# x1 of the second layer multiplied out transposed, 512 tokens at a time, in place of token tiles that are transposed afterwards

## What is computed

```python
q = _lin_lora(x, W[0], A[0], B[0]); k = ...; v = ...      # 4-bit codes looked up and scaled, plus rank 16
attn = (q + k + v) / 3.0
x1 = x + _lin_lora(attn, W[3], A[3], B[3])
g = _lin_lora(x1, Wg, Ag, Bg)
u = _lin_lora(x1, Wu, Au, Bu)
h = jax.nn.silu(g) * u                                     # 1024 x 1792
x = x + attn_block(x)                                      # attn_block returns x1 + d, d = _lin_lora(h, Wd, Ad, Bd)
x = _layernorm(x)
```

## Time and profile before

| | us |
|---|---|
| median of 3 runs | 661.75 (661.51 to 661.8) |
| the profiled execution's own time | 661.55 |
| span of that execution | 659.7 |
| PE busy | 642.2 (97%) |
| DVE busy | 394.1 (60%) |
| ACT busy | 384.2 (58%) |
| POOL busy | 67.5 (10%) |
| mean granted clock of TensorE | 0.996 |

### The profile page before, as it was taken

One profiled execution on the slowest core, in us unless ns is written; L12 is line 12 of the kernel. 1 busy time (PEld: TensorE's weight loads), 2 busy tenths in 40 slices (PEclk: granted clock), 3 DMA queues, 4 the chain that ended last, 5 costly groups with the idle time before them and its releaser, 6 DMA issues.

```text
span 659.7 us, 8518 instructions
## 1 busy us (share of the span) xinstructions
PE 642.2 (97%) x3232; PEld 473.7 (72%) x3232; DVE 394.1 (60%) x622; ACT 384.2 (58%) x528; POOL 67.5 (10%) x117
## 2 busy tenths in 40 slices
PE   9999999999999999999999999999999999999995
PEld 6655455554547778888888888886777888888874
DVE  2778867749688859676766527324675221215566
ACT  3877778866787777766767236213456333226532
POOL 1122213302231000000000000001111000000012
PEclk9999989999999999999999999999999999999999
DMA  6870287522323324332421003038000222100002
GB/s 226 294 269 33 85 267 192 160 80 64 100 99 108 103 70 141 102 108 77 126 79 31 1 0 129 1 113 365 0 5 29 80 97 67 61 1 0 1 32 97
DMA packets 25015, 64.19 MB, mean 97 GB/s; under 512 B 5478, under 2 KB 10022, under 8 KB 24079
## 3 DMA queue, kind: packets, MB, share of 16 engines
q1 hardware_dynamic: 23486, 61.50, 28.9%
q10 hardware_dynamic: 1488, 2.15, 1.0%
HBM read 58.90 MB, written 4.73 MB: 96 GB/s over the span
## 4 chain that ended last, share of the span: by engine, by line
PE 88%; DVE 4%; ACT 4%; issue 2%; POOL 1%; POOLq 0%; ACTq 0%; DVEq 0%
PE bank L1004 19%; PE bank L1083 8%; PE bank L1082 8%; PE bank L991 7%; PE bank L992 7%; PE bank L993 7%; PE bank L766 4%; PE bank L843 4%; PE bank L597 3%; PE bank L716 2%; PE bank L679 1%; PE bank L690 1%; PE bank L631 1%; PE bank L622 1%; PE bank L751 1%
## 5 line engine op out<-in xcount | busy, mean ns | idle before, releaser
L1191 ACT ACTIVATE line<-line 128x1024 f32<-128x1024 f32 x87 | 91.2, 1049 | 0.1
L991 PE MATMUL bank<-xh,wh 128*128 128x512 f32 x224 | 87.5, 391 | 0.0
L992 PE MATMUL bank<-xl,wh 128*128 128x512 f32 x224 | 87.4, 390 | 0.0
L993 PE MATMUL bank<-xh,wl 128*128 128x512 f32 x224 | 87.3, 390 | 0.0
L1004 PE MATMUL bank<-wh,xh 128*128 128x512 f32 x192 | 76.0, 396 | 0.2 <-DVE xl L2082 0.2
L1004 PE MATMUL bank<-wh,xl 128*128 128x512 f32 x192 | 74.9, 390 | 0.0
L2165 DVE SCALAR_TENSOR_TENSOR arena<-bank,ff_s,arena 128x512 f32<-128x512 f32 x28 | 21.0, 751 | 72.9 <-PE bank L1083 63.7
L2082 DVE TENSOR_TENSOR xl<-arena,xh 128x1024 fp32r<-128x1024 f32 (+1 forms) x26 | 29.6, 1141 | 35.2 <-ACT xh L1508 35.0
L1082 PE MATMUL bank<-xh,wh 128*128 128x512 f32 x128 | 50.2, 392 | 0.0
L1083 PE MATMUL bank<-xl,wh 128*128 128x512 f32 x128 | 49.9, 390 | 0.0
L1508 ACT ACTIVATE xh<-arena 128x1024 fp32r<-128x1024 f32 (+1 forms) x26 | 25.6, 991 | 41.3 <-PE bank L1004 34.8
(11 more groups left out here) (211 smaller groups left out, 1276.2 us busy)
## 6 DMA issues: line engine op xcount, KB each, us to landing
codes<-in_c_gu SPq DMA_DIRECT2D x14, 512.0 KB, 3.6
scales<-in_s_gu SPq DMA_DIRECT2D x28, 256.0 KB, 3.8
codes<-in_t_gu SPq DMA_DIRECT2D x8, 512.0 KB, 4.2
codes<-in_c_dn SPq DMA_DIRECT2D x7, 512.0 KB, 5.1
scales<-in_s_dn SPq DMA_DIRECT2D x14, 256.0 KB, 4.0
fold<-in_t_dn SPq DMA_DIRECT2D x1, 3584.0 KB, 16.6
scales<-in_t_gu SPq DMA_DIRECT2D x6, 512.0 KB, 3.7
x<-in_x SPq DMA_DIRECT2D x2, 1024.0 KB, 6.0
```

Source lines behind the costliest of these rows:

```text
L991: pe.matmul(dst, wh[:, s, c:c + P], xh[:, k, cols], start=(k == 0), stop=False)
L992: pe.matmul(dst, wh[:, s, c:c + P], xl[:, k, cols], start=False, stop=False)
L993: last = pe.matmul(dst, wl[:, s, c:c + P], xh[:, k, cols], start=False, stop=(k == KD - 1))
L1191: nc.scalar.activation(below(slot), below(slot), ACT.Prelu, bias=bias, scale=scale, alpha=alpha).then_inc(bent, 1)
```

## The change

x1 is made transposed. The weight is the stationary operand and 512 tokens are the moving one: `x1_T(tg, c)` gives part c of the width for half tg of the tokens, 12 matmuls, into one bank that ACT and DVE read straight into `xh` and `xl`. The copy, the addition and the transposes of x1 go. The rows of x1 are brought back later: `x1_rows_of(b)` multiplies `xh` and `xl` of x1, as stationary operands, with the 128x128 identity in float32r (`unit_r`), into the bank where the down products of tile b are then added: 8 matmuls of 128 columns for each of 8 tiles. `ffn_W(7)` moves to step t = 5. The first two hidden parts of the down stage are worked in halves of the tokens.

```diff
+X1_BANK = ((4, 5, 0, 1), (7, 6, 4, 5))
+FIRST_DN = 2
...
+        unit_r = sb("unit_r", [P, P], F32R)
-        ones = sb("ones", [KD, P])
+        ones = folded_m[0:KD, 0:P]
...
-            def attention_out(t):
...
+            def x1_T(tg, c):
+
+                if tg == 0 and c == 0:
                     pe.wait_ge(m_low, KD)
+                    pe.wait_ge(xl_ready, NT // 2)
+                elif tg == 0 and c == 2:
+                    pe.wait_ge(lmT_ready, NT)
+                elif c == 0:
+                    pe.wait_ge(xl_ready, NT)
+                elif tg and c >= 2:
+                    pe.wait_ge(xl_ready, NT + c - 1)
+                cols, dst = slice(tg * 512, (tg + 1) * 512), bank[X1_BANK[tg][c]][:, :]
                 for k in range(KD):
+                    high, low = m_hi[:, k, c * P:(c + 1) * P], m_lo[k][:, c * P:(c + 1) * P]
+                    pe.matmul(dst, high, xh[:, k, cols], start=(k == 0), stop=False)
+                    pe.matmul(dst, high, xl[:, k, cols], start=False, stop=False)
+                    last = pe.matmul(dst, low, xh[:, k, cols], start=False, stop=(k == KD - 1))
                 last.then_inc(x1_ps, 1)
...
-                if t + 2 < NT - 1:
+                if t + 2 < NT:
                     ffn_W(t + 2)
-                elif t == NT - 1:
-                    ffn_W(t)
...
+                if t == NT - 1:
+                    x1_T(0, 0)
                 lora_out(t)
                 if t >= 2:
                     x_T(2, t - 2)
-            for t in range(2):
-                attention_out(t)
-                x_T(2, NT - 2 + t)
...
+            x1_T(0, 1)
+            x_T(2, NT - 2)
+            x1_T(0, 2)
+            x_T(2, NT - 1)
+            x1_T(0, 3)
+            x1_T(1, 0)
+            gu_lora(0)
+            x1_T(1, 1)
+            x1_T(1, 2)
+            gu_lora(1)
+            x1_T(1, 3)
+
+            def x1_rows_of(b):
+
                 if b == 0:
+                    pe.wait_ge(lora_added, NF)
+                    pe.wait_ge(fold_kept, NF)
+                elif b >= 2 and b % 2 == 0:
+                    pe.wait_ge(h_ready, TG * NF + 1 + b // 2)
+                for k in range(KD):
+                    for m in (xh, xl):
+                        last = pe.matmul(late_bank(b)[:, k * P:(k + 1) * P], m[:, k, b * P:(b + 1) * P], unit_r[:, :], start=(k == 0 and m is xh), stop=False)
+                last.then_inc(x1_rows, 1)
...
+                    if j == NF - 1:
+                        for b in range(NT // 2) if tg == 0 else range(NT // 2, NT - 2):
+                            x1_rows_of(b)
...
-            for j in range(DN_LAST):
+            dn_half(0, 0)
+            for b in range(NT - 2, NT):
+                x1_rows_of(b)
+            dn_half(1, 0)
+            for j in range(FIRST_DN):
+                dn_half(j, 1)
+            for j in range(FIRST_DN, DN_LAST):
                 dn_group(j)
...
+            def x1_T_out(tg, c):
+
+                if c == 0:
+                    act.wait_ge(x1_ps, KD * (tg + 1))
+                nc.scalar.activation(xh[:, c, tg * 512:(tg + 1) * 512], bank[X1_BANK[tg][c]][:, :], ACT.Copy).then_inc(xt_ready, 1)
...
             b_high(0)
             b_high(1)
-            x1_copy(3)
-            x1_T_out(1)
+            for c in range(KD):
+                x1_T_out(0, c)
+            gu_hi(0, 0)
             act.wait_ge(in_gu[1], 16)
             bend_first(C_GU + 1, gu_slot(1))
...
             bend_second(C_GU + 1, gu_slot(1), (scaled, C_GU))
...
+            for n in range(2, LEAD):
+                bend_below(C_GU + 1, gu_slot(1), n)
+            for c in range(KD):
+                x1_T_out(1, c)
             gu_hi(1, 1)
             gu_first_bends(0, 2, 1, (w_ready, 1))
             b_high(2)
...
+            def x1_T_low(tg, c):
...
+                nc.vector.tensor_tensor(xl[:, c, cols], bank[X1_BANK[tg][c]][:, :], f32(xh[:, c, cols]), ALU.subtract).then_inc(xl_ready, 1)
...
             gu_join_above(0, 0)
             b_lower(0)
             b_lower(1)
-            x1_add(2)
-            x1_low(1)
+            nc.vector.tensor_copy(unit_r[:, :], ident[:, :])
+            dve.wait_ge(kb_out, 16 * KD)
+            nc.vector.memset(ones, 1.0)
             gu_to_scale(0, 0, 0)
...
+            for c in range(KD):
+                x1_T_low(0, c)
             gu_lora_add(0, 0)
...
             gu_low(0, 0)
...
             gu_join_above(1, 1)
...
+            for c in range(KD):
+                x1_T_low(1, c)
             gu_to_scale(1, 1, 0)
...
             gu_lora_add(1, 1)
             gu_low(1, 1)
```

More of the change, by code:

```diff
@@ L335, in t_code, with dn_ready @@
             return codes[:, j % SLOTS, :] if j % SLOTS < RING else scales[:, j % SLOTS - RING, :].bitcast(I32)
+        def dn_ready(j):
+            return place(j) + 1 + FIRST_DN
         def place(j):
@@ L396, in decoder_kernel @@
         ag_ps, lm_ready, lm_ps, lmT_ready, f0_ps = (sem(n) for n in ("ag_ps", "lm_ready", "lm_ps", "lmT_ready", "f0_ps"))
-        af_ps, af_added, m_ps, m_high, m_low, x1_ps, x1_ready, x1_sum = (sem(n) for n in ("af_ps", "af_added", "m_ps", "m_high", "m_low", "x1_ps", "x1_ready", "x1_sum"))
+        af_ps, af_added, m_ps, m_high, m_low, x1_ps, x1_rows = (sem(n) for n in ("af_ps", "af_added", "m_ps", "m_high", "m_low", "x1_ps", "x1_rows"))
         gate_ps, up_ps, sil_ready, h_ready = (sem(n) for n in ("gate_ps", "up_ps", "sil_ready", "h_ready"))
@@ L567, in _ @@
             for used, dst, src, done in ((KQ_F, kqT, kq_dram, in_kq), (BETA_F, beta[0:KD, :], beta_dram, in_kq), (CTX_F, ctx1, i["ctx"], in_ctx1)):
-                sp.wait_ge(dn_low, down_ready(used - 1) if used < NF else NF + 1)
+                sp.wait_ge(dn_low, dn_ready(used - 1) if used < NF else NF + FIRST_DN)
                 sp.dma_start(dst, src).then_inc(done, 16)
@@ L943, in gu_lora @@
                 last.then_inc(lora_made, 1)
-            def x1_T(b):
-                pe.wait_ge(x1_ready, b + 1)
-                if b == 0:
[L949 to L967, removed]
+            x1_T(0, 1)
[10 more added lines that the diff above has]
+            def x1_rows_of(b):
+                if b == 0:
+                    pe.wait_ge(lora_added, NF)
[6 more added lines that the diff above has]
+                last.then_inc(x1_rows, 1)
             def gu_tile(s, j):
@@ L1009, in dn_products, with dn_half @@
                 h, l, wh_j, wl_j = hidden_part(xh, j), hidden_part(xl, j), dn_part(wh, j), dn_part(wl, j)
-                return down_products(late_bank(b)[:, :], b, (h, h, l), (wh_j, wl_j, wh_j), j == 0, j == NF - 1)
+                return down_products(late_bank(b)[:, :], b, (h, h, l), (wh_j, wl_j, wh_j), False, j == NF - 1)
             def dn_landed(j):
-                pe.wait_ge(dn_low, down_ready(j))
+                pe.wait_ge(dn_low, dn_ready(j))
                 pe.wait_ge(dn_wlow, place(j) + 1)
+            def dn_half(j, half):
+                pe.wait_ge(dn_low, FIRST_DN * half + j + 1)
+                if not half:
+                    pe.wait_ge(dn_wlow, j + 1)
+                for b in range(half * NT // 2, (half + 1) * NT // 2):
+                    last = dn_products(j, b)
+                if half:
+                    last.then_inc(hu_used, 1)
             def dn_group(j):
-                if j:
-                    dn_landed(j)
+                dn_landed(j)
                 for b in range(NT):
[L1022 to L1030, removed]
                     last = dn_products(j, b)
@@ L1058, in x_scores @@
                     pe.matmul(late_bank(b)[:, 0:P], xT[:, k, t], kqT[:, k, t], start=(k == 0), stop=False)
-                pe.matmul(late_bank(b)[:, 0:P], ones[:, :], beta[0:KD, t], start=False, stop=True).then_inc(x_ps, 1)
+                pe.matmul(late_bank(b)[:, 0:P], ones, beta[0:KD, t], start=False, stop=True).then_inc(x_ps, 1)
             def x_probT(b):
@@ L1437, in _ @@
                 unit_bends(u, h)
-            x1_copy(1)
             x_T_out(3 * NT - 1, dst=xh)
[L1440 to L1444, removed]
+            for u, h in half_plan(3, NT, 1) + half_plan(3, NT + 1, 0) + half_plan(3, NT + 1, 1):
                 unit_bends(u, h)
@@ L1518, in _ @@
             silu(1, NF - 1, 0)
-            act.wait_ge(up_ps, 2 * NF + 1)
-            hidden_hi(hidden_part(xh, 0), 0, HALVES[0], dn_hi)
+            act.wait_ge(x1_rows, NT // 2)
             act.wait_ge(fold_kept, NF)
-            dn_weight_hi(0)
+            for j in range(FIRST_DN):
+                hidden_hi(hidden_part(xh, j), j, HALVES[0], dn_hi)
+                dn_weight_hi(j)
             silu(1, NF - 1, 1)
-            act.wait_ge(up_ps, 2 * NF + 2)
-            hidden_hi(hidden_part(xh, 0), 0, HALVES[1], dn_hi)
-            for j in IN_ORDER[1:]:
+            act.wait_ge(x1_rows, NT)
+            for j in range(FIRST_DN):
+                hidden_hi(hidden_part(xh, j), j, HALVES[1], dn_hi)
+            for j in IN_ORDER[FIRST_DN:]:
                 act.wait_ge(h_ready, TG * (j + 1) + 4)
```

(22 more changed lines are left out.)

48 lines of the change are left out of this document (1 added, 47 removed).

## The result

| | before | after |
|---|---|---|
| median, us | 661.77 | 670.92 (670.03 to 671.56, 4 runs) |
| ratio, 95% interval | | 1.0139 (1.0119 to 1.0159) |
| the profiled execution's own time | 661.55 | 670.03 |
| its span | 659.7 | 668.2 |
| PE busy | 642.2 | 646.6 |

The median is 0.7 us from the forecast of 671.6 and inside the stated range. Of before's four times one, 1660.4 us, is far off the rest; it moves the median by 0.02 us.

The account below looks back on a forecast made before the run. The prediction took PE, working 97% of the span, as the bound, to be checked against the supply of weights. It summed 661.55 + 2.4 (supply and clock) + 7.6 (identity products) = 671.6 us, range 665 to 678.5.

Parts of the forecast that it names:

- Before x1: From lora_T(5) to x_T(2, 7): new waits sum to 2.1 us, like those removed; x_T(2, 7) starts at 209.6 us.
- The x1 stage on PE: 32 transposes go, 3.5 us in all; gate/up starts at 225.4 instead of 229.57, 4.2 us earlier.
- The supply: ACT's and DVE's weight chain into gate/up comes 1.2 us later; PE waits 1.1 us in tile 0, stands 4.8 after it.
- The clock: At gate/up tile 1 PE's stand makes TensorE's clock fall once, 1.8 us lost; net 2.4 us with the supply's shift.
- The row at 85 us: Ground for the fall: clock 0.50 in 85 to 86 us, eight matmuls taking 5.40 us against 3.60.
- Identity products: 64 F32R matmuls of 128 columns added to PE for x1's rows, without cover: 0.118 us each, 7.6 us.
- Gate/up and down: Later gate/up is PE's, so the shift is carried, not made up; the down stage adds nothing.
- The clock stays up: Rival at gate/up tile 1: no clock fall, the shift is 1.2 us, total 670.4 us; chance 0.28.
- PE's saving is kept: Rival for the x1 stage: supply comes before PE, -4.9 us, total 664.3 us; chance 0.10.
- Slow narrow F32R: Rival for the identity products: they cost 14.9 us instead of 7.6, total 678.9 us; chance 0.12.
- products at the price of their columns: Rival: identity products cost only their columns, 3.7 us; chance 0.05 with PE's saving kept, 0.07 with the forecast supply.
- Not slower: Rival: identity products cost 3.7 us; 660.4 us with PE's saving kept (chance 0.05), 666.4 with the forecast supply (0.07).

Follow-up runs that it names:

- e9: e5 with attention_product before ffn_W from step t = 4 on, not step 3, and m_high_of(3) before norm_tail; 660.31 us, ratio 0.9979.
- e3: Changed kernel with b_high(2) ahead of tile 2's bends on ACT and b_lower(2) ahead of join_above on DVE; 671.56 us, ratio 1.0151.
- e4: Changed kernel with the six bends of weight tile 1 ahead of gu_hi(0, 0) on ACT; 666.99 us, ratio 1.0096.
- e5: e4 plus tile 2's bends started before x1's second-half copies, b_high(2) before gu_hi(1, 1), b_lower(2) before gu_join_above(0, 2); 663.14 us, ratio 1.0024.
- e2: Changed kernel with 19 unread 512-column matmuls on PE in the stand at the end of gate/up tile 0; 669.98 us, ratio 1.0130.
- e0: Changed kernel run again unaltered, on the same chip as e5, e7 and e8; 671.29 us, ratio 1.0142.
- e1: Changed kernel with 32 of the 64 identity products, those of x1's low parts left out; 667.14 us, ratio 1.0089.
- e7: e5 with attention_product before ffn_W in all steps and m_high_of(3) before norm_tail; 664.14 us, ratio 1.0041.
- e8: Kernel before the change with attention_product before ffn_W in steps 3 and 4; 664.59 us, ratio 1.0052.

## Why the prediction was right, step by step

**Before x1.** Forecast: waits of 0.8, 0.9 and 0.4 us, `x_T(2, 7)` 2.9 us later. Measured 0.77, 0.54 and 0.48, and 2.5 us. In e9 the first two are gone and nothing takes their place, so they were PE's own; the third is still there in e9 and was not tried.

**The x1 stage on PE.** Forecast 15.8 us from `x_T(2, 7)` to gate/up; measured 16.00. One transpose at 0.108 and a block of 12 at 2.8 us were right.

**The supply.** Forecast: 26.0 us from `x_T(2, 7)` to `gu_hi(1, 1)`. Measured 233.70 - 207.51 = 26.19. The copy to `unit_r` and the memset, which had no row, took 0.23 and 0.17, taken as 0.3. Forecast waits 1.1 and 4.8, measured 0.89 and 4.59. Counted from `lora_T(5)`, the last event that both kernels share, `gu_hi(1, 1)` comes 1.1 us later than before (53.4 us against 52.3), forecast 1.2. This has two parts that the prediction runs together: `x_T(2, 7)` is 2.5 us later, and from there the chain is 1.5 us shorter than before's 27.7 us. The blocks of x1 work on ACT and DVE therefore did not lengthen this chain; they kept it from coming forward with PE, which reaches gate/up 4.3 us earlier. e3 (the stand moves), e4 (it shrinks when ACT's list changes) and e5 (it goes) show that the order of the lists is what holds the supply back.

**The clock.** Right that it falls, and e2 shows that the stand is what makes it fall. The size was a guess from one row (1.8 us of slow matmuls, 1.2 net): `gu_lora(2)` to `down_lora` grew by 2.2 us in one execution and 0.9 in e0. The term was 1.0 us too small for the one and 0.3 too large for the other; how long the clock stays down once PE works again differs between executions. The row at 85 us was a weak ground for the fall itself: PE is busy through 82 to 84 us there, so no stand comes just before it, and in the changed kernel's first execution the same matmuls ran without a fall (1.00 in 84 to 88 us). e2 ties the fall to the stand, that row does not.

**Identity products.** Forecast 0.118 each, 7.6 us; measured 0.112 and, over the rest of the program, 7.0 us (e1: 0.11 each). The transposes (0.108) were the nearer row. What the prediction only argued, that the load of the stationary tile sets this price, a row of its own supports: the 16 one-column matmuls of the earlier trace rows each have a load of their own (least, median and longest ns of one, then the first and the last start):

```profile
L729 PEld LDWEIGHTS bank<-picked,folded x16: 190/192/192, 81.5 to 83.2; 128*128 128x128 f32 x16
L729 PE MATMUL bank<-picked,folded x16: 169/250/250, 81.6 to 83.2; 128*128 128x1 f32 x16
```

With 0.25 us for one they start (1.84 - 0.25)/15 = 0.106 us apart: one column costs as much as 128. These are float32; no run changes the columns of an F32R product alone. The figure of the Trainium skill ("TensorE: Matmul & The Clock Gate", "Back-to-back issue gap"), about 81 ns for load and 128-column matmul, does not hold for the float32 and F32R operands here, with their 0.106 to 0.112 us.

**Gate/up and down.** Nothing is made up or lost there, as forecast: `down_lora` to the end differs by 7.0 us, which the products alone (7.2 by their distance) account for.

**The rivals.** "The clock stays up", 670.4 us, is nearer to the median of 670.92 (0.5 us) than the forecast (0.7); the time could not have told them apart, the trace does. "PE's saving is kept" forecast 664.3; e5, which lets it through, gives 663.14. Slow narrow F32R and products at the price of their columns both fall to e1. The sum of 666.4 under "Not slower" leaves out the forecast's own clock term; with the supply as forecast it would be 661.55 + 2.4 + 3.7 = 667.7.

**The sum.** From `lora_T(5)` to `down_lora` of tile 1 the forecast adds 2.4 us; the first execution added 3.3, e0 2.0. The products were forecast 0.6 too dear. So the mechanism is right, and that the total is right to 0.7 us is in part luck: errors of up to 1 us lie on both sides. The comparison has a flaw as well: the sum was made against an execution that had the early clock fall. Without it the first execution of the changed kernel costs 8.5 + 1.8 = 10.3 us more; e0, which has the fall like before, costs 9.4 more (669.1 against 659.7); the forecast was 10.0 and the medians differ by 9.2.

## What to carry to other kernels

When PE is nearly always busy, look at how much slack its suppliers have before counting a saving on PE: follow their lists from the last common event and compare the two arrival times. An instruction that waits, on an engine that works through its list in order, holds everything behind it, even where the engine's total work falls; here ACT idled 4.8 us with ready work behind (moving six bends into that time returned 3.9 us), and the order of both lists put right returned 8. When each small matmul brings a stationary tile of its own, don't price it by its columns: here 128 columns cost half of 512, and one column as much as 128, so summing by identity products is dear.

## What was not expected of the hardware

A stand of PE of 2.7 us (e4), 3.0 us (e7, e8) or 4.6 us was each time followed by matmuls at half the clock, and 19 matmuls that nobody reads, put into the stand, prevented it (e2). The stand of 4.6 us cost 0.9 to 2.2 us beyond itself, the one of 3.0 us 1.8 (5.40 against 3.60 for eight matmuls). A fall also comes and goes at 84 us between executions with the same waits of PE ahead of it (e0 has the fall, e4 has not); what decides it is not shown, and 1.7 us of a median's scatter can be that alone. And 256 columns of F32R, 128 of F32R, a 128-column float32 transpose and a one-column float32 matmul, each with its own stationary tile, lie within 0.012 us of each other (0.118, 0.112, 0.108, 0.106).
